# A transformer block with two norms: the second norm's product moved from VectorE to ScalarE

## What is computed

```
x = x + tanh(g_xattn) * xattn(layernorm(x), ctx, Wq, bq, Wkv, bkv, Wo, bo)     # 16 heads of 32, 154 keys
x = x + tanh(g_ffn)   * ffn(layernorm(x), w1, b1, w2, b2)                      # hidden 2048, relu, 4-bit-exponent quantizing

def layernorm(x, eps=1e-5):
    m = mean(x); v = var(x)
    return (x - m) / sqrt(v + eps)
```

## Time and profile before

| | |
|---|---|
| median of 3 runs | 1573.12 us |
| lowest, highest | 1571.85, 1573.48 us |
| the profiled execution's own time | 1575.78 us |
| its span, first to last instruction | 1573.9 us |
| mean granted TensorE clock | 0.992 of full speed |
| TensorE busy | 1528.2 us, 97% |
| VectorE, ScalarE, GpSimd busy | 802.0, 818.8, 879.2 us (51, 52, 56%) |

### The profile page before, as it was taken

How to read it: one execution, slowest core, us unless ns; L and a number is a source line. 1 busy time by engine, 2 the same in 40 slices (tenths; PEclk the granted TensorE clock), 3 DMA queues, 4 the chain that set the end, 5 groups by cost and what they waited for, 6 DMA issues and landing times.

```text
span 1573.9 us, 23573 instructions
## 1 busy us (share of the span) xinstructions
PE 1528.2 (97%) x8600; PEld 696.7 (44%) x8600; DVE 802.0 (51%) x1299; ACT 818.8 (52%) x1202; POOL 879.2 (56%) x919
## 2 busy tenths in 40 slices
PE   7877999999999999999999999999999999999998
PEld 4333444444444444444444444444444444444443
DVE  7777364555635455564645556464555646434221
ACT  5755755545455454545546454544645454455421
POOL 3778474654746465474646547464654747445310
PEclk9989999999999999999999999999999999999999
DMA  8446463454434353354444434344444434333120
GB/s 332 110 148 159 162 133 112 134 127 110 121 114 104 124 125 114 105 121 127 111 127 122 115 107 120 113 109 137 126 115 108 123 109 108 99 101 87 44 54 27
DMA packets 252854, 186.69 MB, mean 119 GB/s; under 512 B 160012, under 2 KB 209476, under 8 KB 251076
## 3 DMA queue, kind: packets, MB, share of 16 engines
q1 hardware_dynamic: 252740, 185.19, 42.7%
HBM read 99.95 MB, written 51.59 MB: 96 GB/s over the span
## 4 chain that ended last, share of the span: by engine, by line
PE 91%; SPq 2%; DVE 2%; DMA 2%; ACT 1%; issue 1%; POOL 1%; ACTq 0%; DVEq 0%
PE ring L532 62%; PE ring L745 14%; PE m_ps L638 4%; PE s_ps L668 3%; PE y_ps L696 2%; PE d_ps L685 2%; PE s_ps L661 1%; DMA resid<-in_wo_t 1%; PE y_ps L700 1%; PE d_ps L688 1%; SPq L371 1%; DVE smax L1048 0%; SPq L381 0%; PE ring L574 0%; ACT p L837 0%
## 5 line engine op out<-in xcount | busy, mean ns | idle before, releaser
L532 PE MATMUL ring<-late_a,w 128*128 128x512 f16 (+1 forms) x3096 | 703.9, 378 | 5.6 <-DMA late_a<-x 4.0
L532 PEld LDWEIGHTS ring<-late_a,w 128*128 128x128 f16 x3096 | 302.2, 98 | 346.2 <-issue 11.5
L859 ACT ACTIVATE late_b<-ring,b_sb,wsc 128x512 fp8e4<-128x512 f32 x256 | 199.3, 779 | 434.7 <-PE ring L532 434.7
L1182 POOL TENSOR_TENSOR pmain<-p,pmain 128x512 f16<-128x512 f32 x256 | 308.4, 1209 | 167.8 <-ACT p L837 167.6
L1048 DVE TENSOR_REDUCE smax<-m_ps 128x4 f32<-128x616 f32 x252 | 200.9, 797 | 244.7 <-PE m_ps L638 244.6
L837 ACT ACTIVATE p<-s_ps,prob_log,sc 128x512 f32<-128x512 f32 x320 | 248.0, 775 | 1.5 <-POOL pmain L1182 0.6
L745 PE MATMUL ring<-w,late_b 128*128 128x512 fp8e4 x1024 | 228.2, 379 | 0.9 <-ACT late_b L859 0.9
L834 ACT ACTIVATE pmain<-s_ps,prob_log,sc 128x512 f16<-128x512 f32 x256 | 198.3, 775 | 7.7 <-PE s_ps L668 7.7
L1182 POOL TENSOR_TENSOR pleft<-p,pleft 128x512 f16<-128x512 f32 x64 | 77.2, 1206 | 193.0 <-ACT p L837 192.8
L532 PE MATMUL ring<-wo,yT 128*128 128x512 f16 x768 | 174.5, 381 | 0.0
L532 PE MATMUL ring<-xT,wq 128*128 128x512 f16 x720 | 169.0, 385 | 2.2 <-DVE x L1030 2.2
(11 more groups left out here) (158 smaller groups left out, 1452.7 us busy)
## 6 DMA issues: line engine op xcount, KB each, us to landing
qstack<-q_rows SPq DMA_DIRECT2D x192, 128.0 KB, 3.0
pstack<-left_rows SPq DMA_DIRECT2D x192, 128.0 KB, 2.6
xin<-in_x SPq DMA_DIRECT2D x64, 256.0 KB, 3.4
q_rows<-qparts SPq DMA_DIRECT2D x32, 512.0 KB, 2.8
left_rows<-pleft SPq DMA_DIRECT2D x64, 256.0 KB, 2.5
resid<-in_x SPq DMA_DIRECT2D x64, 256.0 KB, 3.2
out_x<-resid SPq DMA_DIRECT2D x64, 256.0 KB, 2.6
resid<-in_w_t SPq DMA_DIRECT2D x5, 1024.0 KB, 5.4
```

Source lines behind the costliest of these rows:

```text
L532: last = pe.matmul(dst, lhs(a, k), rhs(b, k), start=(k == 0 and p == 0), stop=(k == n_k - 1 and p == 2))
L859: nc.scalar.activation(hT[:, j, :], ring_bank("h", c, j)[:], ACT.Relu, bias=b1_sb[:, j:j + 1], scale=wsc[:, j // 4, 1:2], saturate=False). ...
L1182: nc.gpsimd.tensor_tensor(part[:, 1, :], p32[:, n % 2, :], part[:, 0, :], ALU.subtract).then_inc(prob_lo, 1)
```

## The change

ScalarE makes `xn2` itself, as `Identity(scale * resid + bias)`, directly ahead of its rounding to f16; the scale is the inverse deviation and the bias is minus the mean times the inverse deviation. GpSimd makes this bias in a third tiny step behind the two of `inverse_deviation`, for the second norm only. VectorE's `ln2_apply` and its place in the loop go. The wait for `x2_split` moves with the product to ScalarE. The first norm is left as it was.

```diff
-        rs1 = sb("rs1", [P, TILES, 2], F32)
-        rs2 = sb("rs2", [P, TILES, 2], F32)
+        rs1 = sb("rs1", [P, TILES, 3], F32)
+        rs2 = sb("rs2", [P, TILES, 3], F32)
...
+        ln1_offset, ln2_offset = sem("ln1_offset"), sem("ln2_offset")
...
             def x2_hi(c, t):
+                act.wait_ge(ln2_offset, c * TILES + t + 1)
+                if c + t:
+                    act.wait_ge(x2_split, c * TILES + t)
+                nc.scalar.activation(xn2[:], resid[:, c % 2, t, :], ACT.Identity, bias=rs2[:, t, 2:3], scale=rs2[:, t, 1:2]
+                                     ).then_inc(ln2_done, 1)
                 act.wait_ge(ln2_done, c * TILES + t + 1)
...
-            def ln2_apply(c, t):
-                dve.wait_ge(ln2_rs, c * TILES + t + 1)
-                if c + t:
-                    dve.wait_ge(x2_split, c * TILES + t)
-                nc.vector.tensor_scalar(xn2[:], resid[:, c % 2, t, :], mv2[:, t, 0:1], rs2[:, t, 1:2],
-                                        ALU.subtract, ALU.mult).then_inc(ln2_done, 1)
...
-                run(ln2_apply, LN2_AT, beat, LN2_OWN)
...
-            def inverse_deviation(mv, rs, own, done, count):
+            def inverse_deviation(mv, rs, own, done, count, offset):
                 nc.gpsimd.tensor_scalar(rs[:, 0:1], mv[:, 1:2], LN_EPS, XS ** -2, ALU.add, ALU.mult
                                         ).then_inc(own, 1)
                 pool.wait_ge(own, count)
                 nc.gpsimd.tensor_tensor(rs[:, 1:2], rs[:, 0:1], minus_half[:], ALU.pow).then_inc(done, 1)
+                if offset is not None:
+                    pool.wait_ge(done, count)
+                    nc.gpsimd.tensor_scalar(rs[:, 2:3], mv[:, 0:1], rs[:, 1:2], -1.0, ALU.mult, ALU.mult
+                                            ).then_inc(offset, 1)
```

More of the change, by code:

```diff
@@ L1220, in inverse_deviation @@
                 nc.gpsimd.tensor_tensor(rs[:, 1:2], rs[:, 0:1], minus_half[:], ALU.pow).then_inc(done, 1)
+                if offset is not None:
+                    pool.wait_ge(done, count)
+                    nc.gpsimd.tensor_scalar(rs[:, 2:3], mv[:, 0:1], rs[:, 1:2], -1.0, ALU.mult, ALU.mult
+                                            ).then_inc(offset, 1)
             def ln1_inverse(c, t):
                 pool.wait_ge(ln1_stats, c * TILES + t + 1)
-                inverse_deviation(mv1[:, t, :], rs1[:, t, :], ln1_var, ln1_rs, c * TILES + t + 1)
+                inverse_deviation(mv1[:, t, :], rs1[:, t, :], ln1_var, ln1_rs, c * TILES + t + 1, None)
             def ln2_inverse(c, t):
                 pool.wait_ge(ln2_stats, c * TILES + t + 1)
-                inverse_deviation(mv2[:, t, :], rs2[:, t, :], ln2_var, ln2_rs, c * TILES + t + 1)
+                inverse_deviation(mv2[:, t, :], rs2[:, t, :], ln2_var, ln2_rs, c * TILES + t + 1, ln2_offset)
             def late_biases(n):
```

## The result

| | before | changed |
|---|---|---|
| median of 20 runs each | 1572.03 us | 1574.71 us |
| lowest, highest | 1567.33, 1573.93 us | 1570.84, 1578.41 us |
| the profiled execution's own time, its span | 1575.78, 1573.9 us | 1578.31, 1576.5 us |

The ratio is 1.0022 (95% interval 1.0015 to 1.0030): the changed kernel is 2.4 to 4.7 us slower, 3.5 us in the middle (the two medians alone differ by 2.7 us). The forecast was 1574.4 us, in a range of 1572.3 to 1578.0; the forecast loss was 1.3 us. The time lies in the range and the direction is right, but the loss is larger than forecast and sits on the border of the 0.2% that the prediction called no change; its "slower" had a chance of 0.27. The kernel before has a median of 1572.03 us over 20 runs, 1.1 us lower than the three runs from which the forecast started.

The account below looks back on a forecast made before the run. TensorE was taken as the bound, with no idle time in steady chunks. A loss of 13 x 0.10 = 1.3 us on the median 1573.12 gave 1574.4 us, range 1572.3 to 1578.0.

Parts of the forecast that it names:

- slower: Outcome class for the whole run, beside faster (0.06) and same (0.67); about 0.2%, 3.1 us, counted as no change; chance 0.27.
- The bound: Steady chunk, 493 to 585 us: TensorE busy for all 92.00 us, so savings elsewhere cannot shorten the run, only lateness harms.
- VectorE's freedom: VectorE loses 64 products, 49.2 us: worth nothing by itself, but the fourth tile's residual starts 0.38 us sooner.
- The place: Beat 11's `lift_main` weight load, 0.18 us behind the f32 exponential's end, in 13 chunks: 0.10 us lost each, 1.3 us.
- The two conditions: Fourth tile's ScalarE product waits for GpSimd's bias and for ScalarE's queue behind the attention's cast; both meet at 604.41 us.
- the bias step: GpSimd's third step on one column, 64 times: 0.19 us, up to 0.42; with gap 0.28 each, 18 us if unhidden.
- The product: 64 ScalarE products of 128 x 512: 0.775 us each, taken from an exponential of the same size; skill formula about 0.80.
- The slip: TensorE's weight load 0.31 us late, next matmul 0.23 us behind it: 0.10 us lost per chunk, ends 0 and 0.31.
- Rival 2: GpSimd's third step sets the beat: at 0.27 us 4.4 us in all, at 0.42 us 10 us; chance 0.27.
- the prediction's own signs: Small loss: 13 TensorE waits of 0.1 us; rival 2: waits of 0.3 us and more, fourth product waiting for GpSimd's bias.
- Rival 1: All hidden: ScalarE's product takes the cast's 0.62 us and TensorE loses nothing, 1573.1 us; chance 0.27.
- rival 3: VectorE's freedom pays: without its product blocking GpSimd, the 3.96 us wait at 155.44 could go, 1569.1 us; chance 0.06.

Follow-up runs that it names:

- the kernel with the spare product: Kernel before plus a ScalarE product, later overwritten, ahead of the fourth tile's cast in chunks 1 to 15, VectorE's product kept: steady chunk 92.03 us, ratio 1.0024.

## Why the prediction was right, and where it was too small

The bound. Right: the steady chunk had no time to give and could only be harmed, and VectorE's freedom shortened nothing there (91.67 us without any product).

The place. Right: the exponential ahead of `lift_main` at beat 11, in 13 chunks, with the same 0.24 us in the first twelve and 0.14 us in the last. The second view of the chain, the waits of the weight loads, counts just 13.

The two conditions. Right that they come close to each other. The forecast had both at 604.41, which is 603.56 in the changed kernel's times. The cast's gate came at 603.58, as worked out. GpSimd's gate came at 603.68. The term that failed is the bias step, taken as 0.19 us from the nearest row and measured at 0.267: it enters the queue three times, 3 x 0.08 = 0.2 us, of which 0.12 us stand at the start of the fourth product. The third tile's bias ends at 599.02, 0.22 us behind the forecast's 598.80 (599.65 less 0.85), but the fourth tile's power starts at 602.72, only 0.03 us behind its 602.69. The lo part of the left-over probabilities between them takes 1.16 us, where it took 1.34 us before with VectorE's slow product beside it:

```profile
599.93 1.34 POOL L1182 TENSOR_TENSOR pleft<-p,pleft 128x512 f16<-128x512 f32 x1
```

So VectorE's freedom did give something back, inside the chain and not to TensorE.

The product. Taken as 0.775, measured 0.814: 0.04 us more. The formula of the Trainium skill ("ScalarE: Activation LUTs", section "What ACT_TABLE_LOAD costs") was nearer than the row I preferred.

The slip. The step of the working by which the next matmul comes 0.23 us behind a held load was right: 606.54 to 606.77, and again in the kernel with the spare product (604.90 to 605.13). The loss per chunk is the forecast's 0.10, and 0.14 more from the exponential's end at 606.49 instead of 606.35, of which 0.12 from the product's start and the rest from its length. Over the 13 places that makes 3.0 us instead of 1.3.

So the mechanism and its place held and the size was off by a factor of more than two, since the loss is what is left of an exponential 0.58 us late (606.49 against 606.76 - 0.85 = 605.91) after 0.34 us of slack, and an error of 0.1 us in a term goes straight into it. Rival 2 named the very term and the very value, 0.27 us, and priced it at 0.34 us of loss per chunk and 4.4 us in all: too much, where the forecast was too little. The loss came out at 0.24 us per chunk, just the point from which that rival was said to show. By the prediction's own signs it is rival 2 that came: waits of over 0.3 us (0.56 each, not 0.1) with the fourth product waiting for the bias, a bias step outside 0.19 to 0.22 us, a product outside 0.75 to 0.80 us, and a last cast 0.58 us later in its chunk, not 0.4 to 0.5.

That the time itself, 1574.71 us, came within 0.3 us of the forecast's 1574.4 is in part luck: the starting point, the median of three runs, was 1.1 us above that of 20, which made up most of what the loss was short.

Rival 1, all hidden, is excluded by the 13 waits; rival 3, as a gain, by the kernel without a product.

What stays open: some 0.5 us between the steady part's 3.0 us and the ratio's 3.5 us, well inside its interval.

## What to carry to other kernels

Where the bounding engine has no idle time, ask of a moved step which instruction stands behind it in the new engine's queue and how long before its due time that one ended; here it was 0.18 us, on an engine that was half idle. A step that frees an engine but lengthens a chain through a second engine's in-order queue adds up over the tiles of a chunk, and moving one step of the chain ahead just hands the wait to the next gate, here a single buffer. The cure here was not to make the chain quicker but to issue it behind the work that somebody waits for.

## What the runs showed of the hardware beside this

A tiny GpSimd step whose second factor is read per partition took 0.267 us (median of 64, 0.264 to 0.268), against 0.192 us for the same shape with two constants (median of 128, up to 0.513). In the kernel that kept VectorE's product beside it (0.546 us) it took 0.526 us (median of 64, 0.264 to 0.542). A matmul's weights are loaded ahead: of 0.45 and of 0.57 us by which the load came late, 0.21 us were not lost in both cases.
